# Two gather queues of a four-layer transformer kernel, issued further ahead

## The reference

```
x = x + L1_ffn(layernorm(x))              # mixture of 8 experts, top 2, silu: "routed_out" rows
x = x + L2_xattn(layernorm(x), ctx)       # third attention, 8 heads of 64
x = x + L2_ffn(layernorm(x))              # mixture of 8 experts, top 2, capacity 1024, gelu
x = x + L3_xattn(layernorm(x), ctx)       # single-head self attention, cross attention, small mlp
x = x + L3_ffn(layernorm(x))              # sigmoid gate times squared-relu product
```

## Time and profile before

| | us |
|---|---|
| median of three executions | 1629.52 |
| the profiled execution | 1634.7 |
| its span | 1632.9 |
| PE busy | 1324.6 (81%) |
| DVE busy | 1050.9 (64%) |
| ACT busy | 849.4 (52%) |
| POOL busy | 538.1 (33%) |

### The profile page before, as it was taken

How to read it: one execution, slowest core, us unless ns; L and a number is a source line. 1 busy time by engine, 2 the same in 40 slices (tenths; PEclk the granted TensorE clock), 3 DMA queues, 4 the chain that set the end, 5 groups by cost and what they waited for, 6 DMA issues and landing times. The chain is left out here.

```text
span 1632.9 us, 43718 instructions
## 1 busy us (share of the span) xinstructions
PE 1324.6 (81%) x15232; PEld 1022.8 (63%) x15232; DVE 1050.9 (64%) x3243; ACT 849.4 (52%) x2251; POOL 538.1 (33%) x974
## 2 busy tenths in 40 slices
PE   6999988999499996309999499999469947778887
PEld 3677754655366665308999377777359936556665
DVE  4788847899699998714444466775612226889655
ACT  2566645777577784502222155555124427777565
POOL 4555411111111102770000554564610047662332
PEclk9999995799799997558999799999779977889698
DMA  4432310000000000116767211111123311110001
GB/s 131 146 115 101 112 72 4 14 18 17 12 2 0 0 1 21 49 50 184 205 205 203 67 52 42 48 51 60 41 78 95 118 48 35 36 39 21 1 14 39
DMA packets 99441, 103.95 MB, mean 64 GB/s; under 512 B 11200, under 2 KB 82880, under 8 KB 99136
## 3 DMA queue, kind: packets, MB, share of 16 engines
q1 hardware_dynamic: 71488, 75.37, 14.8%
q0 software_dynamic: 8192, 16.79, 3.6%
q10 hardware_dynamic: 19584, 9.44, 2.0%
HBM read 64.86 MB, written 36.70 MB: 62 GB/s over the span
## 5 line engine op out<-in xcount | busy, mean ns | idle before, releaser
L2475 ACT ACTIVATE e_silu<-e_H 128x256 f32<-128x256 f32 x120 | 42.5, 382 | 163.6 <-DVE e_y L2430 89.7
L2564 PE MATMUL e_H<-e_xT,e_w_up 128*128 128x256 f32 x480 | 112.5, 385 | 0.0
L479 ACT ACTIVATE a_PT<-a_ST 128x1024 f32<-128x1024 f32 x64 | 65.5, 1023 | 77.9 <-PE a_ST L546 77.9
L434 DVE TENSOR_REDUCE a_mx<-a_S 128x8 f32<-128x1024 f32 x64 | 78.1, 1220 | 33.0 <-PE a_S L519 32.8
L2564 PEld LDWEIGHTS e_H<-e_xT,e_w_up 128*128 128x128 f32 x480 | 89.8, 194 | 11.0
L2417 DVE TENSOR_TENSOR e_h<-e_silu,e_H 128x256 f32<-128x256 f32 x120 | 47.6, 419 | 58.6 <-ACT e_silu L2475 58.5
L1412 ACT ACTIVATE a_h<-a_SO,a_w_down 128x256 f32<-128x256 f32 x128 | 50.2, 474 | 65.3 <-PE a_SO L1580 63.0
L519 PE MATMUL a_S<-a_qkM,a_qk 32*128 32x512 f32 x256 | 79.1, 696 | 6.1 <-DVE a_mx L434 6.1
L1328 DVE COPY a_rowsT<-a_pK 128x256 f32<-128x256 f32 x32 | 13.6, 424 | 108.2 <-PE a_pK L1569 108.2
L1353 ACT ACTIVATE a_xT<-a_pQ 128x128 f32<-128x128 f32 (+1 forms) x44 | 14.3, 325 | 119.2 <-PE a_pQ L1442 85.7
L1181 POOL DMA_INDIRECT slots_in<-R,r_put x64 | 63.0, 984 | 36.6 <-DVE r_put L1298 19.4
(11 more groups left out here) (426 smaller groups left out, 4166.9 us busy)
## 6 DMA issues: line engine op xcount, KB each, us to landing
slots_in<-Y SPq DMA_DIRECT2D x32, 512.0 KB, 3.2
e_w_up<-in_f_dram SPq DMA_DIRECT2D x40, 384.0 KB, 3.1
e_w_down<-in_f_dram SPq DMA_DIRECT2D x40, 192.0 KB, 2.9
e_rows<-slots_in SPq DMA_DIRECT2D x40, 128.0 KB, 2.7
slots_out<-e_y ACTq DMA_DIRECT2D x40, 128.0 KB, 2.7
a_rows<-slots_in SPq DMA_DIRECT2D x32, 128.0 KB, 2.1
slots_out<-a_y ACTq DMA_DIRECT2D x32, 128.0 KB, 1.9
W<-in_wpack_dram SPq DMA_DIRECT2D x1, 3276.5 KB, 11.6
```

Of the source, the lines that this page charges most:

```text
L434: nc.vector.tensor_reduce(mx[:, p % 2, 2 * half:2 * half + 2], S[:, :, :].rearrange("p g (h k) -> p g h k", k=D), AX, ALU.max).then_inc(s_ ...
L479: nc.scalar.activation(PT[:, p % 2, 2 * half:2 * half + 2].rearrange("p g h k -> p g (h k)"), ST[:, :, :], ACT.Exp, scale=SCALE).then_inc( ...
L2564: i = nc.tensor.matmul(H[:, banks * p + b, CHUNK * c:CHUNK * (c + 1)], up[:, p, at:at + P], xT[:, p, :], start=True, stop=True)
```

## The change

In the third attention three tiles are gathered before the pipeline starts, and step t gathers one tile or, at every second step, two. Before a gather into semaphore u mod 4, POOL waits until tile u-4 has arrived. In the last stage two pairs are gathered before the pipeline starts, and the gather of pair u+2 is issued at the step after the place of pair u (list entry with lag 1 in place of lag 0); POOL waits likewise for tile t-4.

```diff
+            def gather(u):
+                if u >= IN_FLIGHT:
+                    combine.arrive(pool, u - IN_FLIGHT)
+                combine.gather(u)
+
+            def gather_ahead(u, p):
+                lo = min(3 + u + u // 2, NT)
+                for t in range(lo, min(4 + u + (u + 1) // 2, NT)):
+                    gather(t)
+
+            for t in range(3):
+                gather(t)
             pipeline(pool, NT, [(3, lambda u, p: ln.pool_rstd(pool, u, p)),
-                                (0, lambda u, p: combine.gather(u)),
+                                (1, gather_ahead),
...
-            def gather(u, p):
-                for t in range(2):
-                    combine.gather(2 * u + t)
-
+            def gather(u):
+                for t in (2 * u, 2 * u + 1):
+                    if IN_FLIGHT <= t < NT:
+                        combine.arrive(pool, t - IN_FLIGHT)
+                    if t < NT:
+                        combine.gather(t)
+
+            gather(0)
+            gather(1)
             pipeline(pool, N, [
-                (2, in_self(lambda u, p: n_in.pool_rstd(pool, u, p))), (0, in_self(gather)),
+                (2, in_self(lambda u, p: n_in.pool_rstd(pool, u, p))), (1, in_self(lambda u, p: gather(u + 2))),
```

## The result

The kernel after took **1645.01 us** (median of 7, 1643.29 to 1651.76), the kernel before, run beside it, 1634.46 (1627.96 to 1636.34): ratio **1.009, interval [1.0065, 1.0115]**, slower by 11 to 19 us. Forecast were 1639.5, against a median of 1629.5. The direction was right; the +10.0 was too small.

The account below looks back on a forecast made before the run. POOL's queue was taken to set the third attention's start, PE the rest, and POOL's loop the last stage; +10.7 - 0.5 - 0.2 = +10.0 on the median 1629.5 gave 1639.5 us, range 1631.5 to 1647.

Parts of the forecast that it names:

- The attention's head: Third attention's start: gathers ahead of rstd delay PE's tile 6 and the whole stage by 10.7 us, bounds 7.5 and 14.6.
- PE's own rounds from tile 4 to 6 took 8.49: Third attention's start: PE's own work takes tile 4 at 945.3 to tile 6 at 953.8.
- POOL decides: Third attention, tile 6: POOL's queue allows it at 954.5, just after PE's own 953.8, so POOL sets the time.
- the rule: Third attention: PE takes tile u 1.37 us after rstd(u), else after its own round.
- The waits for tile u-4: POOL's added waits before gathers: landing of 3.53 us hidden behind 7.5 us of issue, cost 0.
- Steps 20 to 31: Third attention's steps without gathers: relief where first scatters and the gather made xn late, -0.5 us, bounds 0 and -1.7.
- Head of the last stage: Last stage's first rounds: nin_rstd(0) to nin_rstd(5) one pair (5.05 us) later, pair 6 some 8 us late.
- The loop: Last stage's interleaved part: period 10.2 us against 10.77 while gathers last, then 9.59; -0.2 for the whole stage.
- B: Loss mostly given back: last stage at DVE's 9.6 (-4.5), scatter relief 1.7; +4.5, 1634 us; chance 0.25.
- D: Faster: DVE running ahead hides POOL's queue, attention loses nothing, last stage gains 10.2; 1619.3 us; chance 0.08.
- E: Change does not do what it says: a tile's rows wait on SBUF still in use; no chance of its own.
- C: PE's clock stays low for tiles 4 and 5 of the third attention, 3.9 more: +13.9, 1643.4 us; chance 0.17.

Follow-up runs that it names:

- e3: Kernel before with third-attention gathers one tile a step to step 11, two from step 12, none ahead of the pipeline; 1628.5 us, executed once.
- e1: Kernel before with the change in the third attention alone, last stage as before; 1650.6 us, ratio 1.0096.
- e5: e1 with six unread matmuls put in PE's step 8, where it waited 3.71 us; 1645.6 us, executed once.
- e8: Kernel before with two third-attention tiles gathered a step at steps 9 to 12 alone; 1637.5 us, executed once; tile 9 5.5 late.
- e4: Kernel before with three third-attention tiles gathered before the pipeline, then one a step, no double steps; 1647.2 us, executed once; tiles 7.5 late.
- e9: Kernel before with the changed attention head, its double steps ended at step 7, then one tile a step; 1646.1 us, executed once; tile 9 13.7 late.
- e6: Kernel before with one pair gathered ahead in the last stage instead of two, attention as before; last stage 302.92 us, executed once.
- e11: e6 again, timed: one pair ahead in the last stage, attention as before; 1631.9 us, ratio 0.9972 to the kernel before, last stage 302.29.
- e7: Kernel before with no last-stage pair ahead; from pair 7, one tile gathered two steps ahead, the other one step ahead; 1629.2 us, ratio 0.9977.
- e10: e9 with four unread matmuls in PE's step 8, before tile 5; 1635.4 us, executed once; tile 9 13.1 late.
- e2: Kernel before with the change in the last stage alone, attention as before; 1634.0 us, ratio 0.9992.

## Why the prediction was wrong in size, step by step
1. **The attention's head, +10.7 forecast, +15.1 measured: the step that failed.** Its first half held: rstd(0) 7.5 late, rounds of 9.1 for two tiles, and tile 4 at rstd(4) + 1.35. What failed is the term "PE's own rounds from tile 4 to 6 took 8.49", and with it "POOL decides" for tile 6. They were not PE's own. Two rows of the kernel before, PE and DVE, that I didn't weigh:
```profile
939.09 0.69 PE L1509 MATMUL a_SO<-a_k,a_q 64*64 64x64 f32 x32 [1.74 <-DVE a_Pr L1217]
```
```profile
935.77 0.35 DVE L247 TENSOR_SCALAR a_xn<-X,a_ln_moments,a_ln_rstd 128x128 f32<-128x128 f32 x1 [1.43 <-issue]
```
PE already waited 1.74 for DVE ahead of tile 5, and DVE 1.43 for rstd(5): tile 5 came 29.55 - 24.67 = 4.88 after rstd(5), the same as after's 4.87 (4.4 to 5.0 in all profiles without filling). Carried forward, tile 5 is at rstd(5) + 4.9 = 42.1, 2.4 above the 39.7 of the rule. The other 2.4 is the clock in the next round (6.46 for 4.06). Tile 6 so stands 4.8 above PE's path, which I had just below POOL's. How much of the 2.4 belongs to the change is open, since e3 lost 1.7 in the same round with the old head; after and e1 both lost 2.4. Further on tile 9 = rstd(10) + 4.3 gives 65.6 by itself; the forecast used rstd(9) and found PE free. The two reach nearly the same height (15.0 and 15.1), so curing the clock alone gains nothing (e5). e8 shows the path through DVE at tile 9 without the rest of the head. That tile 5 of after is held by the same path is read from the rows, and e4, e5, e8 and e9 agree with it; no run changed DVE's order to test it.

2. **The waits for tile u-4, 0.** Held: POOL's rounds are issue alone, 3.3 and 5.8.

3. **Steps 20 to 31, -0.5.** Not there. The delay is 15.1 from tile 9 to tile 31; at the place of the earlier trace rows DVE still waits 1.55 (1061.62 in after) where it waited 1.66, and PE 0.40 where it waited 0.49.

4. **Head of the last stage.** Held: forecast, within the stage, nin_rstd(5) 47.3 and (6) 54.4; measured 47.48 and 54.47. e6 and e11 add what the sum had not asked: the second pair ahead costs 5 to 6 (last stage 308.17 and 307.94 with it, 302.92 and 302.29 without) and brings nothing.

5. **The loop, 10.2.** Held: 10.1 while gathers last, and 9.8 from one nin_shift to the next after them, where 9.59 was forecast; nin_shift(13) is at 126.4, forecast 126.8. The forecast had the gather beside DVE's row additions. It came beside DVE's operations on t_y and W, and kept its long first instruction, 1.20 (the row at 1423.85), while one beside DVE's work on t_pO, at 1383.70, took 1.01. By the Trainium skill, "SBUF — State Buffer", section "Who interferes with whom", a VectorE instruction with two SBUF inputs contends with a GpSimd one that reads SBUF, and one with at most one SBUF input, outside its two-port modes, does not. These two rows fit that rule, but the third instruction of the same gather does not, as it took 0.95 beside both row additions:
```profile
1426.62 0.95 POOL L2650 DMA_INDIRECT Y<-slots_out,r_get  x1 [0.30 <-issue]
```
```profile
1426.73 0.42 DVE L2670 TENSOR_TENSOR X<-X,Y 128x256 f32<-128x256 f32 x1 [0.22 <-ACT R L2663]
```
So the cause of the 0.2 to 0.3 is open.

**The rivals.** B (given back by the last stage) fell: the period is 10.1, and even e7 did not reach 9.6. D and E fell with rstd(0). C, the clock, was right that it costs (2.4) but placed it at tiles 4 and 5, for want of work; there the key matmuls took 1.10 and 1.04. It fell one tile later, after a wait that DVE's order made. C's 1643.4 was nearest for a reason only half its own.

**The base.** The forecast stood on the median of three runs, 1629.5; the seven have 1634.5. Of the 5.5 between 1639.5 and 1645.0 that is 5; the medians differ by 10.6, close to the +10.0. This agreement is luck: the ratio's middle is +14.7, and the stages' sum, where the noise ahead of the attention falls out, is +16.0.

## What to carry to other kernels
Before calling a round "the engine's own", look for idle time inside it and follow what ended it: here a 1.74 wait named a softmax that was itself queued behind the instruction one meant to delay. Issue ahead by as little as takes the landing out of the loop; here each further item ahead was paid in full by what stood behind it in that queue (7.5 for three tiles in e4). In a filling pipeline a late item can cost twice, as time and as a lower clock after the wait.

## What the runs showed of the hardware
- PE's granted clock fell from 1.00 to 0.50 after a wait of 3.71 us (after), and to 0.62 after 3.55 (e8), and stayed at 1.00 where the wait ahead of tile 5 was filled (e5, e10). The round behind it cost 2.4, 1.1 and, in e9 after a wait of 2.24, 1.4 more. A wait of 1.77 was followed by 0.57 and 1.7 more in e3, and one of 1.74 by 1.00 and nothing in the kernel before.
- The same attention code differs by 0 to 1.5 in its head and by 0 to 3 at its end from one execution to another (before, e2, e11), where the clock rises or dips at another place.
- The stages ahead of the third attention, the same in all kernels, took 899.3 to 912.6 us, and the last stage with its old order 306.4 to 308.5. Two single spans that differ by less than 13 say nothing of a change; stage lengths and tile delays do.
